# A decoder block in fp32 on one core: the PV product of cross-attention as fp32 products in four column groups

## What is computed

```python
def proj(x, W, b):
    y = x @ W.T + b
    return y.reshape(B, -1, NUM_HEADS, D_K).transpose(0, 2, 1, 3)
scores = jnp.einsum('bhqd,bhkd->bhqk', Q, K) / math.sqrt(D_K)
scores = jnp.where(mask, scores, jnp.float32(-1000000000.0))
probs = jax.nn.softmax(scores, axis=-1)
attn = jnp.einsum('bhqk,bhkd->bhqd', probs, V)
attn = attn.transpose(0, 2, 1, 3).reshape(B, S, D_MODEL)
return attn @ Wo.T + bo
```

## Time and profile before

| | us |
|---|---|
| median of 3 runs | 888.82 (888.17 to 888.84) |
| the profiled execution | 888.27 |
| its span, first to last instruction | 886.6 |

### The profile page before, as it was taken

One profiled execution on the slowest core, in us unless ns is written; L12 is line 12 of the kernel. 1 busy time (PEld: TensorE's weight loads), 2 busy tenths in 40 slices (PEclk: granted clock), 3 DMA queues, 4 the chain that ended last, 5 costly groups with the idle time before them and its releaser, 6 DMA issues.

```text
span 886.6 us, 18101 instructions
## 1 busy us (share of the span) xinstructions
PE 858.5 (97%) x6299; PEld 778.2 (88%) x6299; DVE 565.3 (64%) x1175; ACT 625.5 (71%) x1772; POOL 308.3 (35%) x355
## 2 busy tenths in 40 slices
PE   8999999999999998999998899999999999999998
PEld 7898999889998986888887789998999999999997
DVE  6898898898889878788887754544223322342223
ACT  5999888878888877989898857654554445444543
POOL 5575564445465766666655520000000000000000
PEclk9999999999999999999999999999999999999999
DMA  6220000000000037646464123200000000000000
GB/s 206 84 61 25 1 1 2 1 2 1 1 26 1 2 101 185 156 110 154 97 144 107 60 74 95 95 13 25 1 1 1 24 0 0 0 24 1 1 1 24
DMA packets 22944, 42.29 MB, mean 48 GB/s; under 512 B 3400, under 2 KB 3920, under 8 KB 22864
## 3 DMA queue, kind: packets, MB, share of 16 engines
q1 hardware_dynamic: 21984, 40.64, 17.1%
q10 hardware_dynamic: 880, 0.60, 0.2%
HBM read 30.36 MB, written 10.49 MB: 46 GB/s over the span
## 4 chain that ended last, share of the span: by engine, by line
PE 82%; DVE 9%; ACT 5%; issue 3%; POOL 1%; POOLq 0%; ACTq 0%; DVEq 0%
PE Y L676 25%; PE A L676 25%; PE S L676 15%; PE T L796 5%; PE O L676 4%; ACT probs L1081 3%; PE O L813 2%; DVE arena L1246 2%; DVE PT L1170 2%; DVE nm L1277 1%; PE O L816 1%; PE S L776 1%; PE S L896 1%; PE S L788 1%; DVE arena L1170 1%
## 5 line engine op out<-in xcount | busy, mean ns | idle before, releaser
L1170 DVE TENSOR_TENSOR PT<-probs,PT 128x512 fp32r<-128x512 f32 x128 | 90.6, 707 | 231.6 <-ACT PT L1150 231.5
L676 PEld LDWEIGHTS Y<-arena,PT 128*128 128x128 f32 x1536 | 199.9, 191 | 11.4 <-DVE PT L1170 1.4
L676 PE MATMUL Y<-arena,PT 128*128 128x256 f32 x1536 | 203.9, 283 | 0.4
L1081 ACT ACTIVATE probs<-S,nm 128x128 f32<-128x128 f32 x512 | 181.9, 377 | 22.7 <-DVE nm L1277 20.4
L1537 POOL TENSOR_TENSOR probs<-probs,rinv 128x512 f32<-128x512 f32 x128 | 133.2, 1041 | 164.6 <-DVE rinv L1282 164.5
L676 PE MATMUL A<-XT,arena 128*128 128x512 f32 x612 | 160.5, 397 | 2.4 <-DVE XT L1209 1.4
L1150 ACT ACTIVATE PT<-probs 128x512 fp32r<-128x512 f32 x128 | 80.8, 631 | 102.2 <-PE Y L676 101.8
L676 PEld LDWEIGHTS A<-XT,arena 128*128 128x128 f32 x612 | 107.8, 189 | 23.4 <-DVE arena L1246 3.9
L1081 ACT ACTIVATION_READ_ACCUMULATOR probs<-S,nm 128x1 f32 x512 | 110.2, 215 | 0.0
L676 PE MATMUL S<-XT,arena 128*128 128x512 f32 x384 | 99.9, 395 | 0.0
L1277 DVE TENSOR_REDUCE nm<-S 128x4 f32<-128x512 f32 x128 | 87.9, 686 | 14.5 <-PE S L676 11.3
(11 more groups left out here) (133 smaller groups left out, 1458.5 us busy)
## 6 DMA issues: line engine op xcount, KB each, us to landing
wst<-in_pieces SPq DMA_DIRECT2D x52, 256.0 KB, 2.6
stage<-arena SPq DMA_DIRECT2D x32, 256.0 KB, 2.3
arena<-stage SPq DMA_DIRECT2D x42, 128.0 KB, 4.2
arena<-stage SPq DMA_DIRECT2D x21, 256.0 KB, 4.0
craw<-in_ctxT SPq DMA_DIRECT2D x4, 512.0 KB, 5.3
out<-craw SPq DMA_DIRECT2D x8, 256.0 KB, 2.3
xs<-in_x SPq DMA_DIRECT2D x3, 512.0 KB, 4.5
arena<-stage SPq DMA_DIRECT2D x6, 96.0 KB, 2.9
```

The source lines that it names most:

```text
L676: mm = pe.matmul(acc, lhs[a], rhs[b], start=first and i == 0, stop=last and i == 2, skip_group_check=shared)
L1081: last = act.activation(probs[:, n % 4, u * P:(u + 1) * P], S[n % 2][:, u * P:(u + 1) * P], ACT.Exp, bias=nm[:, n % 4, u:u + 1], accum_out ...
L1170: dve.tensor_tensor(out_, src, hi.bitcast(F32), ALU.subtract).then_inc(sem_, 1)
```

## The change

Probabilities and V of phase 1 stay whole in fp32. ACT (odd quads) or DVE (even quads) copies T back into `probs`, and the low part is dropped; `v_evac` copies V once into `V2`, which now is the raw weight buffer `wst` itself, and `v_low` is gone. A quad becomes four heads of one batch instead of two heads of two batches: `probs_v` makes four fp32 products, head pair `4 * r + u` onto partitions `32u` to `32u + 31` of O, so that the four stand in four column groups of the array. Two quads of the same batch (`i = n % 8 // 4`) add up the two heads of each pair, and after eight quads all 128 partitions of O are copied in one DVE instruction. `by_pair` permutes the rows of Wq and Wk so that a quad's two stacks hold the right heads.

What follows from that: scores of the first four quads need two stacks (`PAIRS_FIRST = 2`), so `first_keys` and `first_queries` issue 18 DMAs instead of 9 (`KQ_FIRST = 18 * 16`). `exp_probs` of quad n waits for PV of quad n-4, not only for its transposition, because PV reads `probs` itself. `V2` has one buffer, so `v_evac` waits for PV of the last quads of the group before. The first nine experts' raw weights go through three other buffers (two halves of `craw`, and `opart`), the later ones through `wst` after the last PV. POOL clears `wst` once in phase 0 (2048 columns), and its six clearings of `V2` (two of 2048 and four of 1024 columns) go.

```diff
-OUT = Count(0, (16, 8, 0))
-OUT_F1 = Count(1, (16, 8, 0))
+OUT = Count(0, (16, 2, 0))
+OUT_F1 = Count(1, (16, 2, 0))
...
-        V2 = [arena[:, at:at + 4096].rearrange("p (s t u c) -> p s t u c", s=2, t=TILES, u=8)
-              for at in (0, (N1 + N2) * 2 * PIECE)]
...
+        V2 = wst[:, :, :].rearrange("p t (u c) -> p t u c", u=8)
...
+        early = (craw[:, 0:PIECE], craw[:, PIECE:2 * PIECE], opart[:, :])
...
+        def raw_expert(m):
+
+            return early[m % 3] if m < EARLY else wst[:, m % 4, :]
...
             def experts(g):
 
                 for j in range(4):
-                    if isinstance(g, int):
-                        weight_ready(sp, N1 + N2 - 4 + j)
-                    else:
-                        sp.wait_ge(e_split, g * 4 + j - 3)
-                    sp.dma_start(wst[:, j, :], pieces[N1 + N2 + g * 4 + j]).then_inc(w_in[j], 16)
+                    m = 4 * g + j
+                    if isinstance(g, int) and m == EARLY:
+                        sp.wait_ge(pv_ps, nth(SLOT_F2, 1, GROUPS - 1, QUADS - 1))
+                    if not isinstance(g, int) or m >= EARLY:
+                        sp.wait_ge(e_split, m - 3)
+                    elif m >= 3:
+                        sp.wait_ge(e_split, m - 2)
+                    sp.dma_start(raw_expert(m) if isinstance(g, int) else wst[:, j, :],
+                                 pieces[N1 + N2 + m]).then_inc(w_in[j], 16)
...
             def stack_keys(g, r):
 
-                us = slice(g == r == 0, 4)
+                us = slice(PAIRS_FIRST if g == r == 0 else 0, 4)
...
                 for i, s in ((0, 0), (2, 0), (1, 1)):
                     sp.wait_ge((qk_hi, qk_lo)[s], nth((QK, QK_F1)[s], 1, 0, 0))
-                    for h in range(2):
-                        at, to = 16 * h, 32 * i + 16 * h
-                        sp.dma_start(KS[to:to + 16, 0, 0, h, :].bitcast(F32),
+                    for u, h in itertools.product(range(PAIRS_FIRST), range(2)):
+                        at, to = 32 * u + 16 * h, 32 * i + 16 * h
+                        sp.dma_start(KS[to:to + 16, 0, u, h, :].bitcast(F32),
                                      KP[at:at + 16, 0, s, :].bitcast(F32)).then_inc(kq_first, 16)
...
                 for i, s in ((0, 0), (1, 0), (2, 1)):
                     sp.wait_ge((qk_hi, qk_lo)[s], nth((QK, QK_F1)[s], 1, 0, 1))
-                    sp.dma_start(QS[32 * i:32 * i + 32, 0, 0, :].bitcast(F32),
-                                 Q[0:32, 0, s, :].bitcast(F32)).then_inc(kq_first, 16)
+                    for u in range(PAIRS_FIRST):
+                        sp.dma_start(QS[32 * i:32 * i + 32, 0, u, :].bitcast(F32),
+                                     Q[32 * u:32 * u + 32, 0, s, :].bitcast(F32)).then_inc(kq_first, 16)
...
                 if ph == 1 and g == 0 and n == 0:
-                    pe.wait_ge(kq_first, KQ_IN)
-                elif ph == 1 and n % 8 == (2 if g == 0 and n < 8 else 0):
+                    pe.wait_ge(kq_first, KQ_FIRST)
+                elif ph == 1 and n % 8 == (4 if g == 0 and n < 8 else 0):
...
-                    b = 2 * (n % 2) + j
+                    b = 2 * (n % 2) + j if ph == 0 else n % 4
                     acc, at = S[n % 2][:, 256 * j:256 * (j + 1)], slice(b * P, (b + 1) * P)
                     if ph == 0:
                         r = c % 2
                         mm = three(acc, [Q[:, r, s, at] for s in (0, 1)],
                                    [K[:, r, s, b, :, :].rearrange("p h c -> p (h c)") for s in (0, 1)])
                     else:
-                        r, u = c // 4, c % 4
+                        r, u = n // 8, n % 8 // 4 * 2 + j
                         mm = pe.matmul(acc.rearrange("p (h c) -> p h c", h=2), QS[:, r, u, at],
                                        KS[:, r, u, :, at], start=False, stop=True, skip_group_check=True)
...
+                if ph == 0 or n % 8 == 0:
+                    pe.wait_ge(o_sum, nth(OUT_F1, ph, g, (n if ph == 0 else n // 8) - 1))
...
-                    if n < 2:
-                        pe.wait_ge(v_lo, nth(VJ_F1, ph, g, n))
-
+                    if n in (0, 2):
+                        pe.wait_ge(v_lo, nth(VJ_F1, ph, g, n // 2))
+                    r, i, b = n // 8, n % 8 // 4, n % 4
                     for u in range(4):
-                        b, h = 2 * (n % 2) + u // 2, u % 2
-                        mm = three(O[0:32, b * P:(b + 1) * P],
-                                   [V2[g % 2][:, s, b, c, 32 * h:32 * h + 32] for s in (0, 1)],
-                                   [PT[:, n % 2, s, u * P:(u + 1) * P] for s in (0, 1)],
-                                   h == 0, h == 1)
+                        mm = pe.matmul(O[32 * u:32 * u + 32, b * P:(b + 1) * P],
+                                       V2[:, b, 4 * r + u, 32 * i:32 * i + 32],
+                                       probs[:, n % 4, u * P:(u + 1) * P],
+                                       start=i == b == 0, stop=i == 1, skip_group_check=True)
                 mm.then_inc(pv_ps, 1)
...
-                    if g < 2:
-                        act.wait_ge(v_zero, 4 + 4 * g)
+                    if g == 0:
+                        act.wait_ge(v_zero, 1)
                     else:
-                        act.wait_ge(pv_ps, nth(SLOT_F2, ph, g - 2, QUADS - 1))
-                    act.activation(v2(g, 0, job), v2_raw(g, job), ACT.Copy).then_inc(v_hi, 1)
+                        act.wait_ge(pv_ps, nth(SLOT_F2, ph, g - 1, QUADS - 3 + 2 * job))
+                    act.activation(v2(job), v2_raw(g, job), ACT.Copy).then_inc(v_lo, 1)
...
-                act.wait_ge(pt_ps, nth(SLOT_F4, ph, g, n - 4))
+                if ph == 0:
+                    act.wait_ge(pt_ps, nth(SLOT_F4, ph, g, n - 4))
+                else:
+                    act.wait_ge(pv_ps, nth(SLOT_F2, ph, g, n - 4))
...
+                if ph == 1 and n % 2 == 0:
+                    return
                 act.wait_ge(pt_ps, nth(SLOT_F4, ph, g, n))
-                act.wait_ge(pv_ps, nth(SLOT_F2, ph, g, n - 2))
-                act.activation(PT[:, n % 2, 0, :], T[:, :], ACT.Copy).then_inc(pt_hi, 1)
+                if ph == 0:
+                    act.wait_ge(pv_ps, nth(SLOT_F2, ph, g, n - 2))
+                    act.activation(PT[:, n % 2, 0, :], T[:, :], ACT.Copy).then_inc(pt_hi, 1)
+                else:
+                    act.activation(probs[:, n % 4, :], T[:, :], ACT.Copy).then_inc(pt_lo, 1)
...
-                elif n % 4 == 3:
-                    r, at = c // 4, 32 * (c % 4)
-                    act.wait_ge(pv_ps, nth(SLOT_F2, ph, g, n))
-                    act.wait_ge(o_lo, nth(SPLIT_F2, ph, g, r - 2))
-                    act.activation(oraw[at:at + 32, r, :], O[0:32, :], ACT.Identity,
-                                   bias=bias[0:32, BV2 + c:BV2 + c + 1]).then_inc(o_sum, 1)
...
+                if isinstance(g, int) and g == 0 and m < 4:
+                    act.wait_ge(pv_ps, nth(SLOT_F2, 1, GROUPS - 1, QUADS - 4 + m))
...
-                    sub_lo(v2(g, 1, job), v2_raw(g, job), v2(g, 0, job), v_lo)
...
-                dve.wait_ge(pt_hi, nth(SLOT, ph, g, n))
-                sub_lo(PT[:, n % 2, 1, :], T[:, :], PT[:, n % 2, 0, :], pt_lo)
+                if ph == 0:
+                    dve.wait_ge(pt_hi, nth(SLOT, ph, g, n))
+                    sub_lo(PT[:, n % 2, 1, :], T[:, :], PT[:, n % 2, 0, :], pt_lo)
+                elif n % 2 == 0:
+                    dve.wait_ge(pt_ps, nth(SLOT_F4, ph, g, n))
+                    dve.tensor_copy(probs[:, n % 4, :], T[:, :]).then_inc(pt_lo, 1)
...
-                elif n % 4 == 1:
-                    r, at = c // 4, 32 * (c % 4)
+                elif n % 8 == 7:
+                    r = n // 8
                     dve.wait_ge(pv_ps, nth(SLOT_F2, ph, g, n))
                     dve.wait_ge(o_lo, nth(SPLIT_F2, ph, g, r - 2))
-                    dve.tensor_scalar(oraw[at:at + 32, r, :], O[0:32, :], bias[0:32, BV2 + c:BV2 + c + 1],
+                    dve.tensor_scalar(oraw[:, r, :], O[:, :], bias[:, BV2 + r:BV2 + r + 1],
                                       None, ALU.add).then_inc(o_sum, 1)
...
+                if (ph, g, n) == (0, 2, 2):
+
+                    pool.wait_ge(w_low, len(BY_POOL))
+                    pool.wait_ge(w_split, len(BY_DVE))
+                    pool.memset(wst[:, :, :], 0.0).then_inc(v_zero, 1)
...
+    by_pair = np.arange(D).reshape(2, 2, 2, 2, DH2).transpose(0, 3, 1, 2, 4).reshape(D)
```

49 lines of the change are left out of this document (21 added, 28 removed).

## The result

The changed kernel takes **884.03 us** (median of 5 executions, 883.21 to 884.76) against 888.82: a ratio of 0.9948, 95% interval 0.9933 to 0.9962. That is 4.8 us less where 18 were forecast. Faster, but by a quarter of the amount.

What follows compares the result with a forecast made beforehand. PE was taken to bound the kernel, busy 858.5 of 886.6 us. From 888.3, four phase 1 groups save 22.8 (5.7 each) and the opening adds 5.0: 870.5, stated as 871 us; range 855 to 893.

Steps and rivals of the forecast that it cites:

- PV 0.60 us: PE, phase 1: a quad's four fp32 products overlap by halves, taking 0.60 us where PV took 0.72.
- the first rival: PE, phase 1: four column groups overlap fully, PV 0.24 us a quad, ACT becomes the pace, 855 us; chance 0.22.
- the four steps of 0.060: PE, phase 1: each fp32 PV product counted as four steps of 0.060 us, 16 steps a quad.
- Of the 5.5 us of standing still I leave 1.7: PE, each phase 1 group: of 5.5 us standing still or running behind, only 1.7 stays, for 37.3 us a group.
- The full-overlap rival: PE, phase 1: column groups side by side throughout, PV 0.24 us, group 33.4 us, time 855 us; chance 0.22.
- What stands before DVE's copy: DVE, phase 1: waits left are slots where the layer norm stands before the copy of T, 1.7 us a group.
- Busy times: Phase 1 group: ACT falls from 38.5 to 30.9 us, DVE from 35.8 to 27.6; neither can set 43 us.
- The opening, 5.0 us: Start of phase 1: more key and query copies on the SP queue delay PE's first scores, adding 5.0 us, bounds 3 and 6.
- The new wait costs nothing: ACT, phase 1: exponentials waiting for PV of quad n-4 add nothing; ACT has 6.4 us of slack a group.
- The third rival: Phase 1: exponentials' new wait couples ACT to PE, 0.25 us a quad, 16 us of gain lost, about 887; chance 0.14.
- Phase 2 unchanged, expert buffers hidden: Phase 2: stays at 376 us; filling three expert weight buffers, 1.3 us an expert, hides behind PE's 2.9.

## Why the prediction was wrong

- **PV 0.60 us**: the sum holds, the mechanism does not. Products of different column groups run side by side at 7 ns each, as the first rival had it, and as the Trainium skill's page "TensorE: Matmul & The Clock Gate", Part 3, has it with 4 ns. One fp32 product costs 0.217 us, near the four steps of 0.060; I had assumed that the four products overlap only by halves. Against this stood a cost that the sum does not have, 0.29 us a quad for fp32 products of 32 columns between neighbours of 128. Two errors cancelled: 0.58 measured, and 35.3 us of own work a group for 35.6.
- **"Of the 5.5 us of standing still I leave 1.7"**: this is the step that failed. 1.3 of the 5.5 were PE's own work, by the two steps read from different slots, so 4.2 was what could go, and it did not go but grew to 5.3. That is 3.6 us a group more than forecast; with 0.3 less of own work an inner group came out at 40.6 for 37.3. The four groups gained 9.2 for 22.8, and the inner two hold 6.5 of these 13.6 us, the first 5.3 (see the opening), the last 1.8. I argued that the copy's path lost one of its two steps and that ACT had slack, both true. But PE also became faster, so what had arrived in time did not any more: the chain over POOL to the projection had 0.2 us to spare before, which the trace before shows, and it costs 2.0 us of waits a group after. I named only the layer norm as what is late next. The full-overlap rival, which left about half of the 5.5 us, was wrong here too, and in PV's price, 0.24 for a measured 0.58.
- **What stands before DVE's copy**: right in kind, 1.4 us a group and by itself nearly the 1.7 that I left. The layer norm that I named hides behind the projection's wait, as the run with the later projection showed; what delays the copy in the changed kernel are low parts that wait for ACT.
- **Busy times**: ACT 32.2 for 30.9, DVE 28.5 for 27.6. Right that neither sets the group.
- **The opening, 5.0 us**: 4.87, right; the clock was not in the sum. Group 1 gained 0.4 us where the inner ones gained 2.4. Its first interval of scores grew by 1.3 us (4.25 to 5.53), in the stretch of the low clock. A second such stretch, from 350.55 on, cost it 1.3 more, by the run with the query copies first, where the clock stayed up. And its first PV comes at 348.43, in the sixth slot; the slots before it have none that could get shorter, and I should not have given this group the whole gain.
- **The new wait costs nothing**: right, twice, in the changed kernel and without the chains, though the profile puts 8.7 us to it. The third rival's time, 887, lies close to the 884, but its mechanism is not what happened.
- **Phase 2 unchanged, expert buffers hidden**: right, 369.78 us for 369.85.
- What stays open: with both chains out a group takes 38.0 us against some 35.3 of own work. ACT, the DMA and POOL's probabilities account for 1 to 2 us; the rest is spread over steps a few hundredths long, and no run took it apart.

## What to carry to other kernels

When a change takes work from an engine that waits now and then, do not scale its waits down with the work. List every input that arrives just in time over one period, with the time from its source to its use, and compare it with the period you forecast; here one chain of 5.5 us, in time by 0.2 before, cost 2.0 us of waits a group, where the whole change gave 2.4; moving its end gave 1.0 to 1.8 once the other chain was out. A wait named in the profile may lie in the shadow of another one: move one alone and the time can rise, so test them together before you give one up. And leaving work out altogether is the cheapest experiment there is: one product instead of four told in one run that PE's work was not the limit.

## What the runs showed of the hardware

- An fp32 product with 32 standing and 128 moving columns costs 0.217 us in its own column group, and 0.007 us when another group's product runs beside it. It leaves two product records, so a quad shows 8 and not 4.
- Four fp32 products of 32 standing columns between neighbours of 128 cost 0.29 us a quad more than the same at 128 columns, part of it on the instructions before and after, whose own code is unchanged. The transposition's step is 0.36 us in front of fp32r products of 32 columns or of scores, 0.44 in front of fp32 products of 128 columns, 0.53 in front of fp32 products of 32.
- After 4.9 us without work the granted clock fell to 0.58 for 5 us. After a wait of 1.77 us at 484.53 us in the changed kernel the next transpositions took 1.02 us to the next step instead of 0.53, and the granted clock was 0.70 from 480 to 490 us. A short wait can so cost more than itself, but it need not: in the run with the later projection a wait of 1.77 us at 492.28 left the next step at 0.56, and two waits of 1.1 and 1.0 us before 350.55 brought the clock down in the changed kernel, while the same two in the run with the query copies first did not.
